# A graph-attention kernel whose TensorE sums run in an engine loop of two chunks, with a ring of 56 slots, seven sum banks and the self products at the layer's head

## The reference

```python
def _gat_layer(x, src, dst, edge_attr_full, W, att, b, ew, eb):
    edge_emb = edge_attr_full @ ew.T + eb
    xw = x @ W
    xj = xw[src].reshape(-1, H, D) + edge_emb.reshape(-1, H, D)
    xi = xw[dst].reshape(-1, H, D)
    alpha = einsum('ehd,hd->eh', xi, att_i) + einsum('ehd,hd->eh', xj, att_j)
    alpha = leaky_relu(alpha, 0.2)
    amax = segment_max(alpha, dst)
    ea = exp(alpha - amax[dst])
    alpha = ea / (segment_sum(ea, dst)[dst] + EPS)
    aggr = segment_sum(xj * alpha[..., None], dst)
    return aggr.mean(axis=1) + b
for l in range(5):
    h = _gat_layer(h, src, dst, ...)     # with one self edge per node; relu between the layers
```

## Time and profile before

| | |
|---|---|
| device time, median of 3 runs | 3386.26 us (3381.44 to 3386.82) |
| span of the profiled execution | 3764.7 us, 48376 instructions |
| TensorE matmul / weight load busy | 2439.0 / 2001.4 us |
| DVE, ACT, POOL busy | 2004.0, 696.7, 2210.5 us |
| mean granted TensorE clock | 0.537 |

### The profile page before, as it was taken

How to read it: one execution, slowest core, us unless ns; L and a number is a source line. 1 busy time by engine, 2 the same in 40 slices (tenths; PEclk the granted TensorE clock), 3 DMA queues, 4 the chain that set the end, 5 groups by cost and what they waited for, 6 DMA issues and landing times.

```text
span 3764.7 us, 48376 instructions
## 1 busy us (share of the span) xinstructions
PE 2439.0 (65%) x13595; PEld 2001.4 (53%) x13595; DVE 2004.0 (53%) x6216; ACT 696.7 (19%) x3102; POOL 2210.5 (59%) x2357
## 2 busy tenths in 40 slices
PE   6779726666582766658276665837576582766668
PEld 6679615555461655547165554725455461655546
DVE  8955624554472555547255554725454472555456
ACT  0078511111121111112111111211111121111112
POOL 0067466666626766662666666266676626666661
PEclk8555555555565555556555555655555565555556
DMA  3212122222202222221222222022222202222221
GB/s 101 97 60 80 30 52 54 53 52 57 49 24 51 54 51 53 56 49 30 47 54 52 53 56 49 25 53 54 50 53 57 50 24 50 54 50 53 52 49 40
DMA packets 114121, 195.78 MB, mean 52 GB/s; under 512 B 39897, under 2 KB 77272, under 8 KB 113864
## 3 DMA queue, kind: packets, MB, share of 16 engines
q0 software_dynamic: 62560, 130.25, 15.2%
q1 hardware_dynamic: 51304, 62.42, 5.3%
HBM read 180.86 MB, written 11.67 MB: 51 GB/s over the span
## 4 chain that ended last, share of the span: by engine, by line
DVE 36%; PE 25%; another core or an unknown queue 20%; issue 13%; DVEq 3%; POOL 1%; ACT 1%; ACTq 1%; DMA 0%; POOLq 0%
PE bank L745 10%; PE bank L747 6%; DVE acc L1200 4%; DVE into L1143 2%; DVEq L1016 2%; PE bank L718 2%; DVE pw L1161 2%; DVE alpha L1094 2%; PE bank L741 2%; PE bank L783 2%; DVE fwd L1150 2%; DVE lanes L1129 2%; DVE prod L1072 1%; PE bank L766 1%
## 5 line engine op out<-in xcount | busy, mean ns | idle before, releaser
L510 POOL DMA_INDIRECT ring<-table,srci x1955 | 1941.2, 993 | 937.6 <-issue 556.4
L745 PE MATMUL bank<-pw,ring 128*128 128x48 f32 x3910 | 1210.9, 404 | 203.3 <-issue 201.8
L745 PEld LDWEIGHTS bank<-pw,ring 128*128 128x128 f32 x3910 | 1014.9, 314 | 302.9 <-issue 231.1
L1200 DVE TENSOR_TENSOR acc<-acc,bank 128x288 f32 x490 | 222.8, 455 | 1128.7 <-remote 857.3
L747 PE MATMUL bank<-onehot,est 128*36 128x24 f32 x3910 | 632.6, 243 | 222.9 <-issue 221.7
L741 PE MATMUL bank<-zeros 128*128 128x288 bf16 x490 | 208.5, 426 | 697.1 <-DVE pw L1161 438.7
L747 PEld LDWEIGHTS bank<-onehot,est 128*36 128x36 f32 x3910 | 391.2, 149 | 393.9 <-issue 226.6
L741 PEld LDWEIGHTS bank<-zeros 128*128 128x128 bf16 x490 | 55.4, 113 | 752.0 <-DVE pw L1161 453.3
L586 ACT ACTIVATE dd<-dd 128x66 f32<-128x66 f32 x75 | 19.4, 258 | 2163.4 <-DVE dd L1154 1177.9
L580 ACT COPY ai_win<-ai_rows 128x48 f32 x1955 | 336.3, 229 | 432.6 <-issue 410.5
L491 POOL TENSOR_TENSOR ring<-ring,acc 128x512 f32<-128x512 f32 x98 | 117.1, 1195 | 250.1 <-ACT ring L545 246.7
(11 more groups left out here) (214 smaller groups left out, 2610.1 us busy)
## 6 DMA issues: line engine op xcount, KB each, us to landing
ring<-table,srci POOLq DMA_INDIRECT x1955
ai_rows<-lo_dram SPq DMA_DIRECT2D x28, 896.0 KB, 4.3
at<-in_attr SPq DMA_DIRECT2D x65, 224.0 KB
table<-ring SPq DMA_DIRECT2D x15, 390.0 KB, 3.5
table<-ring SPq DMA_DIRECT2D x5, 325.0 KB, 3.4
result<-ring SPq DMA_DIRECT2D x24, 64.0 KB
x_mid<-ring SPq DMA_DIRECT2D x3, 384.0 KB, 2.7
table<-ring SPq DMA_DIRECT2D x5, 130.0 KB, 2.4
```

The source lines that it names most:

```text
L510: nc.gpsimd.indirect_dma_start(out=ring[:, slot(t), :], out_offset=None, in_=table, in_offset=bass.IndirectOffsetOnAxis(ap=srci[:, t:t + 1 ...
L745: nc.tensor.matmul(wide[:, 0:H, at_k], ring[:, slot(t), 0:D], pw[:, g % DEEP, k, :, :], start=False, stop=False, skip_group_check=True)
L1200: V.tensor_tensor(win, win, grp_sum(g).rearrange("p (r w) -> p r w", r=REG), ALU.add)\
```

## The change

TensorE's first twelve chunks of a layer are no longer written out. They run as a loop on TensorE's sequencer (`nc.tensor.Fori`) of six passes, and one pass does two chunks, 14 groups. For the loop's body to be the same instructions in each pass, what was a constant has to repeat every two chunks or come from the loop's register: the ring has 56 slots (two chunks) instead of 60, there are seven sum banks (one for each group of a chunk) instead of six, with as many buffers for the weighted one-hots `pw`, the one-hot's address is computed from the register, and `p_ready` is two semaphores, one for each chunk of the pair, which TensorE clears after a chunk's last wait. Bank 3 stays no sum bank; the seventh is bank 7. The 25 self products move to the layer's head, after `ai_product` and ahead of the loop, through banks 0 to 3, and DVE takes them out there, ahead of its first `windows_sum`. The scratch `hi_mask` of the stage before the layers moves to another buffer. The last 14 groups of a layer stay written out.

```diff
-RING = 60
+RING = 56
+PAIR = 2 * K
+PAIRS = 6
+LOOPED = PAIRS * PAIR
+SELF_BANKS = 4
-SUM_BANKS = (0, 1, 2, 4, 5, 6)
+SUM_BANKS = (0, 1, 2, 4, 5, 6, 7)
...
-            def aggregate(layer, g):
-                c, t0, n = GROUPS[g]
-                gg = layer * G + g
+            def aggregate(half, b, i, start, start_w, place, n, closes):
+                t = start + place
                 _, off = nc.values_load_multi_w_load_instructions(
-                    offs[0:1, t0 + 1:t0 + n], engines=(mybir.EngineType.PE,), min_val=0, max_val=GW - WIN,
+                    offs[0:1, bass.ds(t + 1, n - 1)], engines=(mybir.EngineType.PE,), min_val=0, max_val=GW - WIN,
                     skip_runtime_bounds_check_because="clamped on the chip")
-                pe.wait_ge(p_ready, gg + 1)
-                if g == 3:
-                    for h in range(H):
-                        pe.wait_ge(ai_sb[h], NQ * (layer + 1))
-                    pe.wait_ge(tr_sb, NQ * (layer + 1))
-                total = grp_sum(g)
+                pe.wait_ge(p_ready[half], i + 1)
+                if closes:
+                    pe.sem_clear(p_ready[half])
+                total = grp_sum(b)
...
-                    nc.tensor.matmul(wide[:, 0:H, at_k], ring[:, slot(t), 0:D], pw[:, g % DEEP, k, :, :],
+                    nc.tensor.matmul(wide[:, 0:H, at_k], ring[:, slot(place + k), 0:D], pw[:, b, k, :, :],
                                      start=False, stop=False, skip_group_check=True)
-                    ins = nc.tensor.matmul(wide[0:EC, H, at_k], est[:, c % 2, t - TC[c], :], onehot[:, t, :],
+                    ins = nc.tensor.matmul(wide[0:EC, H, at_k], est[:, half, i * GRP + k, :],
+                                           onehot_tw[:, bass.ds(start_w + (place + k) * WIN, WIN)],
...
-                def self_tile(j):
-                    if j:
-                        pe.wait_ge(s_sb, n + j)
-                    nc.tensor.matmul(bank[3][:, 0:H * D + H], S[:, j, D:2 * D],
+                for j in range(NT):
+                    if j >= SELF_BANKS:
+                        pe.wait_ge(s_sb, n + j - SELF_BANKS + 1)
+                    nc.tensor.matmul(bank[j % SELF_BANKS][:, 0:H * D + H], S[:, j, D:2 * D],
                                      Wl[:, layer % 2, :], start=True, stop=True).then_inc(s_ps, 1)
-
-                for c in range(NC):
-                    for i, g in enumerate(GC[c]):
-                        aggregate(layer, g)
-                        if s_tile_of(c, i) is not None:
-                            self_tile(s_tile_of(c, i))
+                for h in range(H):
+                    pe.wait_ge(ai_sb[h], NQ * (layer + 1))
+
+                with nc.tensor.Fori(0, LOOPED, PAIR) as start:
+                    start_w = nc.tensor.snap(start * WIN, min_val=0, max_val=(LOOPED - PAIR) * WIN)
+                    for half in range(2):
+                        for i in range(DEEP):
+                            aggregate(half, i, i, start, start_w, half * K + i * GRP, GRP, i == DEEP - 1)
+                for g in range(2 * PAIRS * DEEP, G):
+                    c, t, k = GROUPS[g]
+                    aggregate(c % 2, g % DEEP, GC[c].index(g), LOOPED, LOOPED * WIN, t - LOOPED, k, g == GC[c][-1])
...
                 for q in range(NQ):
                     ai_copy(V.tensor_copy, v, layer, q, 1)
+                for j in range(NT):
+                    self_rows(j)
...
-                        if s_tile_of(c, i) is not None:
-                            self_rows(s_tile_of(c, i))
```

More of the change, by code:

```diff
@@ L64 @@
 assert TC[NC] == REAL and RING >= SHIFT + NT
+PAIR = 2 * K
+PAIRS = 6
+LOOPED = PAIRS * PAIR
+SELF_BANKS = 4
+assert PAIR == RING and all(k == K for k in CH[:2 * PAIRS])
 def slot(t):
     return (t + SHIFT) % RING
-def s_tile_of(c, i):
-    n = 3 * c + i // 2
-    return n if c < 9 and i % 2 == 1 and i < 6 and n < NT else None
 def pool_group(g):
@@ L84 @@
 AHEAD = 4
-SUM_BANKS = (0, 1, 2, 4, 5, 6)
+SUM_BANKS = (0, 1, 2, 4, 5, 6, 7)
 DEEP = len(SUM_BANKS)
+assert DEEP == K // GRP and G % DEEP == 0
 def chain_at(c):
@@ L174, in program @@
         hT = prod[:, 0:P]
+        onehot_tw = onehot[:, :, :].rearrange("p t w -> p (t w)")
         xt = ring[:, 0:NT, :]
@@ L232, in program @@
         parts = part(rowsf, 2 * 4 * PC, BF16).rearrange("p (b q t) -> p b q t", b=2, q=4)
-        hi_mask = part(rowsf, NT * PC, BF16).rearrange("p (h t) -> p h t", h=NT)
         n_parts = part(rowsf, 3 * NT, BF16).rearrange("p (q h) -> p q h", q=3)
@@ L261, in program @@
         b2s = ai_win[:, :, :, :].rearrange("p k h w -> p (k h w)")[:, D:2 * D]
+        hi_mask = ai_win[:, :, :, :].rearrange("p k h w -> p (k h w)")[:, 2 * D:2 * D + NT * PC // 2]\
+            .bitcast(BF16).rearrange("p (h t) -> p h t", h=NT)
         bank = [ctx.enter_context(nc.psum_tensor(f"bank{i}", [P, 512], F32)) for i in range(8)]
@@ L341, in program @@
         exp_al = sem("exp_al")
-        p_ready = sem("p_ready")
+        p_ready = [sem(f"p_ready{i}") for i in range(2)]
         sums = sem("sums")
@@ L742, in aggregate @@
                 for k in range(n):
-                    t = t0 + k
                     at_k = bass.ds(off[k - 1], WIN) if k else slice(0, WIN)
-                    nc.tensor.matmul(wide[:, 0:H, at_k], ring[:, slot(t), 0:D], pw[:, g % DEEP, k, :, :],
+                    nc.tensor.matmul(wide[:, 0:H, at_k], ring[:, slot(place + k), 0:D], pw[:, b, k, :, :],
                                      start=False, stop=False, skip_group_check=True)
-                    ins = nc.tensor.matmul(wide[0:EC, H, at_k], est[:, c % 2, t - TC[c], :], onehot[:, t, :],
+                    ins = nc.tensor.matmul(wide[0:EC, H, at_k], est[:, half, i * GRP + k, :],
+                                           onehot_tw[:, bass.ds(start_w + (place + k) * WIN, WIN)],
                                            start=False, stop=k == n - 1, skip_group_check=True)
@@ L1163, in weigh @@
                                 est[:, c % 2, k:k + n, HF:HF + H].unsqueeze(3).broadcast_to((P, n, H, WIN)), ALU.mult)\
-                    .then_inc(p_ready, 1)
+                    .then_inc(p_ready[c % 2], 1)
             def chain_probs(layer, c):
@@ L1214, in self_rows @@
                     v.wait_ge(s_ps, n + j + 1)
-                    V.tensor_copy(node_ai[:, :, j], bank[3][:, H * D:H * D + H])
-                    V.tensor_tensor(S[:, j, :], bank[3][:, 0:H * D], ebl[:, :], ALU.add)\
+                    V.tensor_copy(node_ai[:, :, j], bank[j % SELF_BANKS][:, H * D:H * D + H])
+                    V.tensor_tensor(S[:, j, :], bank[j % SELF_BANKS][:, 0:H * D], ebl[:, :], ALU.add)\
                         .then_inc(s_sb, 1)
```

## The result

The changed kernel takes 3393.18 us, median of 17 runs (3388.8 to 3396.77). The kernel before took 3386.65 us beside it (17 runs, 3381.44 to 3387.92). The ratio is 1.0019, with a 95% interval from 1.0013 to 1.0025: 6.5 us slower, which is a little less than the 0.2% that I had called "about what can be told from none", but the interval leaves out 1.

A forecast was written before the change was run, and what follows sets the result against it. POOL's gathers were taken as the bound: 475.5 + 5 x (505 + 89.2) = 3446 us, less 60 unplaced, is 3386; every part of the change adds 0, so 3386 us, 8-in-10 range 3360 to 3415.

The forecast's parts named there:

- What bounds the kernel: All layers: POOL's 391 gathers pace each, 505 us, plus 89.2 us at its end; recorded ring waits, 63 us, not real.
- 60 that I can't place: Whole kernel: 3446 us by the trace's durations without waits, against the measured 3386; 60 us taken off without a place.
- the part without gathers isn't 89 us: End of a layer, where no gather runs: any length other than 89 us would show the model of the bound wrong.
- The self products leave the chunks: In the chunks: TensorE loses 25 x 1.02 us, DVE 25 x some 0.5 us; both wait anyway, so effect 0.
- They come to the head: Layer's head: 25 products take 13 us, or 25.5 us at half clock, hidden behind chunk 0's gathers; exposure 0.
- The ring: POOL's gathers: with 56 slots first wait at 72 us, group 0 summed by 60 us at most; margin 12 us, cost 0.
- the seventh bank: TensorE's sum banks: DVE's weigh runs at most four groups ahead, so six were enough; effect 0.
- The loop: TensorE's first twelve chunks: a pass takes 47.7 to 50 us against POOL's 72.2, branch back 1 to 3 us hidden; effect 0.
- Ring waits that are real: POOL's gathers: up to 63 us a layer really lost, 5 x 25.5 = 128 us given back, 3259 us; chance 0.13.
- A late head: Layer's head: group 0 comes after 72 us, so four slots fewer cost 5 us a layer, 3411 us; chance 0.12.
- A slow loop: TensorE's loop: branch back over 11.6 us or pass over 72 us; uncovered, 3 us x 30 give 3475 us; chance 0.09.
- 391 gathers still at 1.29 us: POOL in the profile after: a layer's gathers should each still take 1.29 us; closer together would show the model wrong.

The follow-up runs named there:

- e1: The kernel before, unchanged, profiled a second time: 3387.66 us, span 3385.9 us instead of the first recording's 3764.7.
- e5: The changed kernel with unused stand-in work on DVE, the size of the self rows, behind groups 1, 3 and 5 of the chunks: 3393.71 us, 1.0009 to the kernel before.
- e8: The changed kernel with unused stand-in work on DVE behind group 5 of the chunks only: 3405.72 us, 1.0041 to the kernel before.
- e2: The kernel before with only the self products and self rows moved to the layer's head: 3392.41 us against 3387.5, ratio 1.0013.
- e4: The changed kernel with the twelve chunks written out instead of looped: 3392.32 us, 1.0018 to the kernel before.
- e7: The changed kernel with unused stand-in work on DVE behind groups 3 and 5 of the chunks: 3386.09 us, 0.9984 to the kernel before.
- e11: The changed kernel with ACT copying edge attributes into PSUM after its windows, read there by DVE's product est alone: 3316.01 us, 0.9788 to the kernel before.
- e12: The kernel before with ACT copying edge attributes into PSUM bank 7 after its windows, read there by est alone: 3316.16 us against 3387.45, ratio 0.9788.
- e3: The kernel before with only the ring of 56 slots and hi_mask in another buffer: 3386.98 us, ratio 0.9999.
- e6: The changed kernel with unused stand-in work on DVE behind group 1 of the chunks only: 3398.48 us, 1.0022 to the kernel before.

## Why the prediction was right or wrong

**What bounds the kernel** was right in kind: POOL's gathers pace the layer, and TensorE's late sums in the earlier trace rows belonged to that one recording (e1). It was wrong in a number that looked harmless: "391 gathers need 386.1 + 390 x 0.305 = 505 us, 1.29 us each" took a gather's time for a property of the gather. Undisturbed it takes 0.945 us and the pause 0.305, so 1.25 us; the mean of the earlier trace rows, 386.1 / 391 = 0.987, holds 0.04 us of DVE's doing. In the second profile of before the mean is 1.002 us, and over 1955 gathers 1955 x 0.057 = 111 us of POOL's time are this excess, nearly all of it beside the four products of the table under e5 to e8. Read one by one, the gathers of 1.3 us and more beside DVE's products stand out; a mean, and the four short ones of the earlier trace rows (0.94 to 0.97 us), hide them.

The second profile also places the "60 that I can't place". A layer's gather part is 510.6 us and not 505, 28 us more over five layers, and a layer's end is 71.4 us and not 89.2, 89 us less. The two errors of the sum had opposite signs, and it came to 3386 us only because the measured median was put in; so the likeliest time's nearness to 3393 says nothing for the terms. That "the part without gathers isn't 89 us" was one of the prediction's own signs of a wrong model, and it was there.

**The self products leave the chunks.** Here the prediction failed: "Freed time on an engine that waits anyway: 0". The engine does wait anyway, and nobody waits for it, but DVE's products with two SBUF operands hold up POOL's gathers, and taking some 0.5 us of DVE's work out ahead of one changes when it does. The term put at nothing measured: the gathers take 11.2 us more, the end of the first layer gives back 4.6, and 6.5 us are left. e2, which moves only the self rows, has it (4.9 us); e4, without the loop, has it (4.8 us); e7, which puts work back behind the groups 3 and 5, takes it away (0.9984); e11 and e12, in which `est` no longer collides, make both kernels equal.

The Trainium skill names such a collision (SBUF — State Buffer, section Who interferes with whom): a DVE instruction with two SBUF inputs and a GpSimd instruction that reads SBUF share a read port, which the first comer holds for its whole length. The trace agrees, in that the gather goes on only when the product has ended, and in that one operand in PSUM frees it (0.94 us); the product keeps its 1.08 us whichever starts first. The same section infers that making a DMA's descriptors isn't stalled by such a product; here the gathers, which read their row numbers `srci` from SBUF, are (0.94 us undisturbed, 1.34 to 1.77 in the rows above), and the measurement decides. That it is this port, and not something else that the two share, is argued from the operands, not shown.

**They come to the head.** Right: TensorE had been at work on the head's products, the granted clock is 1.00 (2.4 GHz), and the 25 products take 11.0 us (I had 13, at 0.92). Group 0 starts 47 to 48 us after the layer's first gather and is summed 3.4 us later (I had at most 60), and 9.49 us of DVE's wait are left. This stretch (window, length, PE, PEld, DVE, ACT and POOL busy, granted clock, DMA share, GB/s):

```profile
1070.00:1079.50 9.50, 9.01 (x42) 7.54 (x40) 9.50 (x45) 3.44 (x23) 7.14 (x8) 1.00 0.27 58
```

**The ring** and **the seventh bank**: 0, as said (e3; no wait in the profile after).

**The loop**: 0, as said (e4 against the changed kernel: ratios 1.0018 and 1.0019). My price for a branch back, "1 to 3 us a pass", was too high: its rows show 0.21 us. q8 carried 66 packets where it was 122 before, and in no layer did one start between the loop's first branch back and its end (in layer 1 the packets start at 1157.9 and 1557.3 us, the branches at 1164.7 to 1533.3): a body of 602 instructions, 38.5 KB by my estimate, was not fetched again. The rule by which all 30 branches stall (the Trainium skill, Runtime: NRT & Kernel Launch, section Instruction fetch mechanics) isn't borne out here.

**The rivals.** Ring waits that are real (3259 us): no, by e1. A late head (3411 us): no, group 0 is summed some 51 us after the first gather and the ring asks for it at 72 to 73, so some 21 us are to spare. A slow loop (3475 us): no, by e4 and the branch's rows. (Two slips in the sums change nothing: 1.02 us at 0.50 is 0.55 us at 0.92 and not 0.51, and 3 us x 30 is 90 and not 89; besides, only 25 of the 30 branches go back.) The right case, a slowdown through POOL's own instructions, was not among them; I had only listed as a sign that "391 gathers still at 1.29 us" should hold, and that is the sign that broke (512.9 us a layer for them instead of 510.6).

What stays open: why the first recording was slow; why the phases of e2, e5 and e6 come out as they do, which the table reads off but doesn't derive; and whether the 4.6 us in the first layer's end come from the change or differ from one execution to the next (e2 has 71.5 us there, e3 72.7, e4 71.6).

## What to carry to other kernels

Where one engine paces a kernel by many equal instructions, look at the spread of their durations and not at the mean: the long ones name an engine that isn't on the path and still costs time. Here work moved or added on such an engine changed the time from -0.16% to +0.41% against the kernel before, and not in the order of its amount, so a small gain or loss after moving it says nothing of the move, until the collision is taken away and both versions are timed again. And a wait that only the recording shows should be recorded a second time before anything rests on it.

## What the runs showed of the hardware that I had not expected

- A product on DVE with both operands in SBUF holds up an indirect DMA's instruction on POOL that starts during it, until 0.82 us after the product's end, 0.40 to 0.82 us more in the rows above. With one operand in PSUM it doesn't, and a copy of that operand into PSUM by ACT, which has the time, takes 71 us off the kernel before (3387.45 to 3316.16), less than half of it at the product itself (29 us) and the rest where the next products then fall.
- A loop body of 602 instructions ran six times a layer on TensorE with no packet on its instruction queue after the first pass, and a branch back took 0.21 us.
- The same program was recorded once with a span of 3764.7 us and once with 3385.9, the first time with waits that the second doesn't have.
